# A three-layer fp32 model on one Trainium2 core: norms of the head-attention stage moved to GpSimd, and side work dealt out to other steps

## The reference

```
x = x + attn_a(layernorm(x))   # gated attention, quadratic and linear parts, width 256
x = x + ffn(layernorm(x))      # mixture of experts
x = x + attn_b(layernorm(x))   # 16 heads of 64: the "head attention"
x = x + ffn(layernorm(x))      # the same mixture of experts, same weights

layernorm: (x - mean) / sqrt(var + 1e-5)

attn_b:  q, k, v = x @ w + b (per head); attn = softmax(q k^T / 8, axis=2)
         out = concat(attn @ v) @ l_w.T + l_b

ffn:     probs = softmax(x @ Wr); the two best of 8 experts for each token
         each expert takes the first 160 tokens of a batch row that chose it
         h = relu(slots @ W1 + b1); y = h @ W2 + b2
         out = sum over the two of prob * kept * y[slot of the token]
```

## Time and profile before

| what | value |
|---|---|
| median of 3 runs | 1502.43 us (1499.57 to 1503.81) |
| span of the profiled execution | 1499.3 us |
| mean granted clock of TensorE | 0.993 of full speed |
| PE busy | 1445.1 us, 96% |
| DVE busy | 1063.7 us, 71% |
| ACT busy | 919.5 us, 61% |
| POOL busy | 280.3 us, 19% |

### The profile page before, as it was taken

How to read it: one execution, slowest core, us unless ns; L and a number is a source line. 1 busy time by engine, 2 the same in 40 slices (tenths; PEclk the granted TensorE clock), 3 DMA queues, 4 the chain that set the end, 5 groups by cost and what they waited for, 6 DMA issues and landing times.

```text
span 1499.3 us, 43267 instructions
## 1 busy us (share of the span) xinstructions
PE 1445.1 (96%) x18426; PEld 1004.5 (67%) x18426; DVE 1063.7 (71%) x2172; ACT 919.5 (61%) x1727; POOL 280.3 (19%) x325
## 2 busy tenths in 40 slices
PE   7999789999999999999999999999999999999996
PEld 6988774565677675656777756557777565467486
DVE  6884037887666679877666788776667887777754
ACT  5765566656666666566666666666666665666553
POOL 4165613013210012130000120400000213000055
PEclk9999999999999999999999999999999999999999
DMA  8501221001110011010000110110001101100002
GB/s 223 192 19 57 67 61 38 22 23 46 28 30 16 16 42 33 23 48 16 16 16 16 40 32 22 34 47 16 16 16 39 32 23 34 47 16 16 1 19 57
DMA packets 44461, 58.27 MB, mean 39 GB/s; under 512 B 8231, under 2 KB 32656, under 8 KB 44144
## 3 DMA queue, kind: packets, MB, share of 16 engines
q1 hardware_dynamic: 35120, 38.27, 9.4%
q0 software_dynamic: 9152, 17.26, 4.1%
HBM read 22.14 MB, written 19.32 MB: 28 GB/s over the span
## 4 chain that ended last, share of the span: by engine, by line
PE 86%; DVE 7%; ACT 3%; issue 2%; another core or an unknown queue 2%; DMA 0%; DVEq 0%; ACTq 0%
PE bank L1134 29%; PE bank L1147 26%; PE bank L1057 6%; PE bank L1062 4%; PE bank L1071 3%; PE bank L434 3%; PE bank L406 3%; DVE nmx L1169 3%; PE bank L1289 2%; PE bank L1285 2%; ACT prob L1178 2%; PE bank L1246 1%; ACT hT L528 1%; DVE stats L1330 1%
## 5 line engine op out<-in xcount | busy, mean ns | idle before, releaser
L1178 ACT ACTIVATE prob<-bank,nmx 128x1024 f32<-128x1024 f32 x512 | 570.3, 1114 | 427.3 <-DVE nmx L1169 426.4
L1169 DVE TENSOR_REDUCE nmx<-bank 128x1 f32<-128x1024 f32 x512 | 625.8, 1222 | 210.2 <-PE bank L1134 193.7
L1147 PE MATMUL bank<-prob,vsc 64*64 64x512 f32 x4096 | 644.9, 590 | 4.6 <-DVE ctxT L1196 2.7
L1134 PE MATMUL bank<-q,k 64*64 64x512 f32 x2048 | 530.4, 592 | 6.6 <-ACT prob L1178 5.5
L1134 PE MATMUL bank<-q,ks 64*64 64x512 f32 x2048 | 527.4, 591 | 0.0
L1147 PEld LDWEIGHTS bank<-prob,vsc 64*64 64x64 f32 x4096 | 232.3, 133 | 130.6 <-issue 64.3
L1057 PE MATMUL bank<-xT,wqkv_sb 64*64 64x256 f32 (+1 forms) x1560 | 210.3, 435 | 0.0
L1134 PEld LDWEIGHTS bank<-q,ks 64*64 64x64 f32 x2048 | 137.0, 133 | 81.0 <-issue 26.8
L1741 POOL DMA_INDIRECT yg<-yslots,row_ring x64 | 64.5, 1008 | 609.3 <-PE bank L1134 581.5
L1134 PEld LDWEIGHTS bank<-q,k 64*64 64x64 f32 x2048 | 133.9, 133 | 46.8 <-ACT prob L1178 16.6
L1057 PEld LDWEIGHTS bank<-xT,wqkv_sb 64*64 64x64 f32 x1560 | 90.3, 133 | 89.3 <-issue 39.7
(11 more groups left out here) (270 smaller groups left out, 1619.7 us busy)
## 6 DMA issues: line engine op xcount, KB each, us to landing
ks<-k SPq DMA_DIRECT2D x62, 256.0 KB
yslots<-slots_sb SPq DMA_DIRECT2D x7, 640.0 KB, 3.6
slots_sb<-xslots SPq DMA_DIRECT2D x5, 640.0 KB, 4.8
xslots<-xhat_r POOLq DMA_DIRECT2D x5, 512.0 KB, 7.3
yslots<-xhat_r POOLq DMA_DIRECT2D x5, 512.0 KB, 12.4
w_sb<-in_w SPq DMA_DIRECT2D x1, 2048.0 KB, 9.0
wqkv_sb<-in_wqkv SPq DMA_DIRECT2D x1, 2048.0 KB, 19.1
xslots<-xhat_r,row_s POOLq DMA_INDIRECT x112
```

Of the source, the lines that this page charges most:

```text
L1134: ins = nc.tensor.matmul(bank[rows(c), SC[h][n], :], kk[r, cols(2 * j + c, HD)], qst[pi % 2][r, cols(n, HALF)], start=True, stop=True)
L1147: ins = nc.tensor.matmul(bank[rows(h), CX[n], :], vsc[s][rows(r), rows(h)], prob[g % 3][h][rows(r), cols(n, HALF)], start=(j == 0 and firs ...
L1169: nc.vector.tensor_reduce(nmx[:, 2 * s + h:2 * s + h + 1], bank[:, SC[h][0]:SC[h][0] + 2, :], mybir.AxisListType.XY, ALU.max, negate=True) ...
L1178: nc.scalar.activation(prob[g % 3][h][:].rearrange("p (n c) -> p n c", c=HALF), bank[:, SC[h][0]:SC[h][0] + 2, :], ACT.Exp, bias=nmx[:, 2 ...
```

## The change

- The Newton steps and the normed rows of both norms (except the c norm of row 0) run on GpSimd, in `norm_gpsimd`: four operations a round on 128 x 8, three rounds, eight TENSOR_SCALAR of 128 x 128, and for a c norm the bias addition of 128 x 1024. VectorE keeps statistics, aggregation and the first guess, in four steps of three, three, two and no tiles.
- The c norm of row 1 has its statistics at steps 24 to 27 of block 0, those of rows 2 and 3 at steps 0 to 3 of blocks 1 and 2. The f norms begin at step 0 of block 0 and step 8 of the others.
- Chunks: in blocks 1 to 3 `xr`, `lg`, `pos` are one step later; `ln` is at steps 36 and 37 of block 0 and 9 and 10 of blocks 1 and 2; the experts begin at step 38 of block 0 and 37 of the others, and the last `answers` of block 0 is at step 0 of block 1. `slots` moves one step later in blocks 1 and 2.
- Combines: one tile a step at steps 38 to 53 (two a step in block 0).
- GpSimd's indirect DMAs: scatters and the first gathers are each held by the scores of one head, so that two in one step are half a step apart; the later gathers are at the steps in `GATHER_AT`, and the norms stand between them in GpSimd's program.

```diff
+        ROUTE_AT = [13, 14, 14, 14]
+        LN_AT = [36, 9, 9]
+        SLOTS_AT = [33, 34, 34]
+        EXPERTS_AT = [38, 37, 37]
+
         def chunks_of(b):
-            out = {13: ("xr", 0), 14: ("xr", 1), 15: ("lg", 0), 19: ("pos", 0)}
-            if b < B - 1:
-                out.update({28: ("ln", 0), 29: ("ln", 1)})
+            r = ROUTE_AT[b]
+            out = {r: ("xr", 0), r + 1: ("xr", 1), r + 2: ("lg", 0), r + 6: ("pos", 0)}
             if b == B - 1:
                 return out
+            for i in range(2):
+                out[LN_AT[b] + i] = ("ln", i)
             for i in range(3):
-                out[33 + i] = ("slots", i)
-                out[60 + i] = ("answers", i)
+                out[SLOTS_AT[b] + i] = ("slots", i)
+                out[EXPERTS_AT[b] + 3 * E + i] = ("answers", i)
             for e in range(E):
-                out[36 + 3 * e], out[37 + 3 * e], out[38 + 3 * e] = ("up", 2 * e), ("up", 2 * e + 1), ("down", e)
+                at = EXPERTS_AT[b] + 3 * e
+                out[at], out[at + 1], out[at + 2] = ("up", 2 * e), ("up", 2 * e + 1), ("down", e)
...
+                if pi % PAIRS == 0 and pi > 0:
+                    v.wait_ge(n_bias, b)
...
+        def c_bias_vector(v, step):
+            xb = xres[:, 0:T, :]
+            v.wait_ge(m_xhat, 2)
+            step.done(nc.vector.tensor_tensor(xb, xb, bl_sb[:].unsqueeze(1).to_broadcast([P, T, P]), ALU.add))
+
+        def first_norm_vector(v, step, piece):
+
+            if piece == 0:
+                aggr_vector(v, step, T)
+                newton_vector(v, step, T, NEWTON, True)
             else:
+                xhat_vector(v, T, 0, xhat, piece - 1, m_xhat)
+
+        NORM_ORDER = [("f", 0), ("c", 1), ("c", 2), ("f", 1), ("c", 3), ("f", 2), ("f", 3)]
+
+        def norm_vector(v, step, kind, b, piece):
+
+            c0, row = (T, b) if kind == "c" else (0, (b - 1) % B)
+            if piece == 0 and kind == "f" and b > 0:
+                v.wait_ge(c_res, 2 * PAIRS * b)
+            if piece < 3:
+                stats_vector(v, step, c0, row, ((0, 1, 2), (3, 4, 5), (6, 7))[piece])
+            if piece == 2:
+                aggr_tiles(v, step, c0, range(4))
+            if piece == 3:
+                aggr_tiles(v, step, c0, range(4, T))
+                guess_vector(v, step, c0)
+
+        def aggr_tiles(v, step, c0, tiles):
+            step.wait()
+            for t in tiles:
+                ins = nc.vector.bn_aggr(meanvar[:, c0 + t, :], stats[:, c0 + t, :])
+            step.done(ins)
+
+        def guess_vector(v, step, c0):
+            c = slice(c0, c0 + T)
+            step.wait()
+            step.then(nc.vector.tensor_scalar(varp[:, c], meanvar[:, c, 1], EPS, None, ALU.add))
+            step.done(nc.vector.tensor_scalar(half_var[:, c], varp[:, c], -0.5, None, ALU.mult))
+            step.then(nc.vector.tensor_scalar(newton[:, c].bitcast(I32), varp[:, c].bitcast(I32), 1, None, ALU.arith_shift_right))
+            nc.vector.tensor_tensor(rstd[:, c].bitcast(I32), magic[:, c], newton[:, c].bitcast(I32), ALU.subtract).then_inc(n_guess, 1)
...
+        def norm_gpsimd(p, step, kind, b):
+
+            c0, row, xh, done = (T, b, xhat, m_xhat) if kind == "c" else (0, (b - 1) % B, xhat_r, g_xhat)
+            c = slice(c0, c0 + T)
+            y, z = rstd[:, c], newton[:, c]
+            hold(p, n_guess, NORM_ORDER.index((kind, b)) + 1)
+            for _ in range(NEWTON):
+                step.then(nc.gpsimd.tensor_tensor(z, y, y, ALU.mult))
+                step.then(nc.gpsimd.tensor_tensor(z, z, half_var[:, c], ALU.mult))
+                step.then(nc.gpsimd.tensor_scalar(z, z, 1.5, None, ALU.add))
+                step.then(nc.gpsimd.tensor_tensor(y, z, y, ALU.mult))
+            if kind == "f" and b > 0:
+                p.wait_ge(g_sc, 256 * b)
+            elif kind == "f":
+                p.wait_ge(f_sc, 256 * (B - 1))
+            elif b == 1:
+                p.wait_ge(m_xT, 2)
+            else:
+                p.wait_ge(g_free, ln_turned(b - 2))
+            for t in range(T):
+                ins = nc.gpsimd.tensor_scalar(xh[:, t, :], row_of(row, t), meanvar[:, c0 + t, 0:1], rstd[:, c0 + t:c0 + t + 1],
+                                              ALU.subtract, ALU.mult)
+                if t % 4 == 3:
...
+                    ins.then_inc(done, 1)
+            if kind == "c":
...
+                p.wait_ge(m_xhat, 2 * (b + 1))
+                nc.gpsimd.tensor_tensor(xb, xb, bl_sb[:].unsqueeze(1).to_broadcast([P, T, P]), ALU.add).then_inc(n_bias, 1)
...
-        COMBINE = {14: (0, 0, 4), 15: (0, 4, 8), 31: (1, 0, 4), 32: (1, 4, 8)}
-        COMBINE_0 = {5: (1, 0, 0, 4), 6: (1, 0, 4, 8), 14: (1, 1, 0, 4), 15: (1, 1, 4, 8),
-                     43: (2, 0, 0, 4), 46: (2, 0, 4, 8), 52: (2, 1, 0, 4), 55: (2, 1, 4, 8)}
+        FIRST_COMBINE = {}
+        for n, at in enumerate((6, 8, 9, 10, 11, 12, 13, 14)):
+            FIRST_COMBINE[at] = (1, n // 4, 2 * (n % 4))
+        for n, at in enumerate((42, 43, 44, 45, 50, 51, 52, 53)):
+            FIRST_COMBINE[at] = (2, n // 4, 2 * (n % 4))
+        COMBINE_AT = 38
+        NORM_AT = {}
+        for kind, b, at in (("f", 0, 0), ("c", 1, 24), ("c", 2, 64), ("f", 1, 72), ("c", 3, 128), ("f", 2, 136), ("f", 3, 200)):
+            for piece in range(4):
+                NORM_AT[at + piece] = (kind, b, piece)
...
+            if b == 0 and s in FIRST_COMBINE:
+                fb, k, t = FIRST_COMBINE[s]
+                first_combine_vector(v, step, fb, k, (t, t + 1))
+            if b > 0 and COMBINE_AT <= s < COMBINE_AT + 2 * T:
+                k, t = divmod(s - COMBINE_AT, T)
+                f_combine_vector(v, step, b, k, (t,))
+            if g in NORM_AT:
+                norm_vector(v, step, *NORM_AT[g])
+            r = s - ROUTE_AT[b]
+            if 3 <= r < 6:
+                f_route_vector(v, step, b, r - 3)
+            if 7 <= r < 9:
+                f_route_vector(v, step, b, r - 4)
...
-                if s == 31:
+                if s == SLOTS_AT[min(b, B - 2)] - 2:
...
-                if s == 63 and b < B - 1:
-                    hold(sp, g_free, chunk_at(b, 62) + 1)
-                    sp.dma_start(yslots[slots, :].rearrange("(i p) c -> p i c", p=P), slots_sb[:]).then_inc(g_st, 16)
-                if s == 35 and b >= 2:
+                if g - 1 in CHUNK and CHUNK[g - 1][1:3] == ("answers", 2):
+                    n, fb = CHUNK[g - 1][0], (CHUNK[g - 1][3] - 1) % B
+                    hold(sp, g_free, n + 1)
+                    sp.dma_start(yslots[fb * SLOTS:(fb + 1) * SLOTS, :].rearrange("(i p) c -> p i c", p=P), slots_sb[:]).then_inc(g_st, 16)
+                if s == COMBINE_AT + 2 * T + 1 and b >= 2:
...
-        def paced(p, g):
-
-            hold(p, c_qk, 2 * min(g + 3, LAST + 1))
+        def paced(p, g, h=1):
+
+            hold(p, c_qk, 2 * min(g + 3, LAST + 1) - 1 + h)
+
+        GATHER_AT = [3, 4, 6, 7, 8, 9, 10, 11, 14, 15, 16, 17, 18, 19, 20, 21]
...
-                        paced(p, 31 + c)
-                    elif t % 2 == 0:
-                        paced(p, 1 + c // 2)
+                        paced(p, 33 + c)
+                    else:
+                        paced(p, 1 + c // 2, c % 2)
...
-                    elif b < B:
-                        paced(p, g0 + k * T + t)
                     c = k * T + t
+                    if b < B:
+                        if c == 2 and b < B - 1:
+                            norm_gpsimd(p, step, "c", b + 1)
+                        if c == T:
+                            norm_gpsimd(p, step, "f", b)
+                        paced(p, b * STEPS + GATHER_AT[c])
...
-                    if t % 2 == 0:
-                        paced(p, b * STEPS + 22 + (k * T + t) // 2)
+                    c = k * T + t
+                    paced(p, b * STEPS + ROUTE_AT[b] + 9 + c // 2, c % 2)
...
+        def c_gpsimd(p, step):
             first_gather(p, 1)
+            norm_gpsimd(p, step, "f", 0)
             for b in range(B - 1):
                 c_scatter(p, b)
                 if b == 0:
+                    norm_gpsimd(p, step, "c", 1)
                     first_gather(p, 2)
-                c_gather(p, b + 1, range(2))
+                c_gather(p, step, b + 1, range(2))
             c_scatter(p, B - 1)
```

More of the change, by code:

```diff
@@ L1228, in chunk_wait @@
         def chunk_wait(pe, g):
-            b = g // STEPS
-            n, kind, i = CHUNK[g]
+            n, kind, i, b = CHUNK[g]
             if kind == "xr":
@@ L1621, in c_vector @@
             nc.vector.tensor_scalar(bq, bq, HD ** -0.5, None, ALU.mult).then_inc(c_bias, 1)
-            c_norm_vector(v, step, 0, 7)
+            c_bias_vector(v, step)
             for h in range(2):
@@ L1723, in beside_last, with c_gather @@
                 hold(p, f_ytr, 3 * m + i - 4)
-        def c_gather(p, b, ks):
+        def c_gather(p, step, b, ks):
             fb = (b - 2) % B
@@ L1732, in c_gather @@
                 hold(p, f_st, 16 * (B + 1))
```

(10 more changed lines are left out.)

74 lines of the change are left out of this document (10 added, 64 removed).

## The result

The changed kernel takes 1,486.96 us (median of 4 runs, 1,483.37 to 1,490.19), the kernel before on the same chip 1,501.0 (4 runs, 1,499.25 to 1,503.81): ratio 0.9903, 95% interval 0.988 to 0.9926, so 14 us faster. The forecast was 1,491.8, its own range 1,489 to 1,494.5, the wide range 1,483.5 to 1,499.5.

A forecast was written before the change was run, and what follows sets the result against it. TensorE was taken to bound the head-attention stage, leaving only small holes to win; 7.5 + 1.2 + 4.2 - 2.3 = 10.6 us gained gave a median of 1,491.8, own range 1,489 to 1,494.5, 8-in-10 range 1,483.5 to 1,499.5.

The forecast's parts named there:

- So of the 4.2, scatters explain 1.7 and the c norm 2.5: Steps 22 to 30, blocks 0 to 2: hole of 4.2 us; moving norm work off VectorE gains 7.5 in all.
- Indirect DMAs one by one, half of 8.4: Scatters and first gathers: paired DMAs cost 8.4 us at present; spacing them gains half, +4.2.
- rival 1: Spaced indirect DMAs cost what paired ones do; 6.4 us gained, so 1,496.0; chance 0.20.
- Combines and `xr` a step later, 0.3 a block: Steps 14 and 15 lose four combine operations each on VectorE; 0.3 us a block, 1.2 gained.
- the routing pieces cost what they cost: Routing pieces move one step with the `xr` chunk in blocks 1 to 3, at no added cost.
- The bias addition, three hits of half of 1.4, -2.3: GpSimd's three long bias additions may hold back VectorE's `vsc`; about half of 1.4 us each, -2.3.
- GpSimd's rows at 0.29: Each 128x128 norm row on GpSimd takes 0.29 us, interpolated between 0.19 and 0.61.
- Rival 5: Norm rows come late for the transposes; at three times the path's time, 4 us late in three blocks, 1,504; chance 0.02.
- Steps 22 to 30 near 40: Sign: this stretch of blocks 0 to 2 falls to near 40 us from 44.
- Rival 3: The c norm's 2.5 is TensorE's lost pairing from any disturbance, not VectorE's load; 3.1 us gained, 1,499.3; chance 0.10.
- Rival 4: GpSimd keeps the ports through a burst, so `vsc` waits out rows and bias; slower, 1,510; chance 0.08.
- Rival 2: Everything goes: bias additions miss `vsc`, spaced DMAs are free; 17.1 us gained, 1,485.3; chance 0.15.

The follow-up runs named there:

- the split: Changed kernel with GpSimd's 128x1024 bias addition cut into eight of 128x128, without waits between; 1,456.03 us, ratio 0.9975 to the kernel before.

## Why the prediction was right, point by point

The direction and the wide range held, but two errors of opposite sign met in the sum; that it came out this near is luck. In the stage, 13.2 us were gained where 10.6 were forecast. By the two kinds of chip this divides into 10.8 from spacing (forecast +4.2) and 2.4 from all the rest (7.5 + 1.2 - 2.3 = 6.4), if the rest is worth as much on the one chip as on the other.

- *"So of the 4.2, scatters explain 1.7 and the c norm 2.5"*: this is the step that failed. It took the scatters' cost from block 3 and called the remainder the c norm's. The same program without late maxima has 40.53 for 43.96 in block 1 and 38.80 for 40.65 in block 3: bursts cost 3.4 in the one and 1.85 in the other. That a late maximum meets less room with the c norm beside it is my reading of the difference, not shown. The c norm, dense on VectorE but without its `ln` chunks in the stretch, costs 1.05 in three blocks, not 7.5. With them it costs more: on the chip without late maxima block 1's stretch is 1.73 longer than block 3's (40.53 and 38.80). The two `ln` chunks take 0.93 of that, by steps 9 and 10 of the changed kernel there (4.77 and 4.76 in block 1 with them, 4.30 each in block 3 without); 0.8 a block is left, 2.4 in three. Pairs have no part in it: with single DMAs the stretch is 40.53 too.
- *Indirect DMAs one by one, half of 8.4*: the present cost was mis-sized (the stage of the same program is 14.6 shorter where nothing is late; I had 8.4), and so was the part of it that goes: 10.8, not half. In the changed kernel single DMAs leave no maximum over 0.13 late in two traces of such chips. So rival 1, which had single ones as late as paired ones, is refuted, and my bound of 24 us lost was far off. I had looked at maxima only: what single DMAs do cost here, at most the 3.8, shows on TensorE in the step traced above.
- *Combines and `xr` a step later, 0.3 a block*: steps 13 to 15 did get 0.96 to 1.1 a block shorter, but not by the combines: with routing back at 13 and the combines still gone they take 15.22. They got shorter because the `lg` chunk left them for step 16, which I had not followed: steps 16 to 21 grew by 1.8, and steps 13 to 21 of the four blocks are 2.45 longer. The term was nothing, and "the routing pieces cost what they cost" was wrong. That the position of the routing does it, the run with routing at 13 shows. 0.5 a block of it is TensorE's late start beside the gather of step 16; the rest I did not trace.
- *The bias addition, three hits of half of 1.4, -2.3*: two hits, 1.75 by the split. Right. (Three times half of 1.4 is 2.1, not 2.3.)
- *GpSimd's rows at 0.29*: 0.80. The interpolation between 0.19 and 0.61 failed; GpSimd needs 2.2 times VectorE's 0.359. The Trainium skill, "GPSIMD Engine Reference", section 4.1, calls one-input operations roughly line-rate and only two-input ones twice as slow; here the one-input row is even more so than the two-input bias (2.37 to 1.22, 1.9 times). It cost nothing: the first four rows, which TensorE asks for first, end 2.0 later than I had them, and of the 5.4 to spare 3.4 were left in block 1. Rival 5 had no part.
- *Steps 22 to 30 near 40*: they came to 38.9. My floor of 39.8 held two ln chunks, and the change sends these to steps 36 and 9; that is 0.8 of the fall, and it is given back there (steps 0 to 12 of block 1 +1.2, 36 to 63 of block 0 +0.9).
- *Rival 3* (TensorE's lost pairing, set off by any disturbance) was nearer the truth on the norm than my forecast, as to the price: with VectorE as busy as before, the stretch is short once the bursts and the `ln` chunks are gone. Its mechanism was not tested. *Rival 4*: the rows hold `vsc` by 0.2 at most (0.47 for 0.29, once).
- *Rival 2* fits the time best, by compensation: bias additions did not miss `vsc`, but sending the DMAs singly was worth more than it assumed.

What stays open: why one chip starts its engines late behind indirect DMAs and another doesn't. The instructions, the DMAs' durations and the granted clock in the stage (1.00) are the same. The experiments saw two chips of the one kind and one of the other, each once, so that it is the chip, and not something else about that set of runs, is not shown. Nor was spacing alone run in the kernel before, or pairs in the changed one, on a chip where it matters; the 10.8 is a difference of differences.

## What to carry to other kernels

When a stretch is long beside two suspects, price each by a kernel that has only that one; the remainder after subtracting the first is not the second's price when both use the same room. Send indirect DMAs of GpSimd one by one between the steps of other engines: a single one cost about 0.5 us in a few steps where the result was measured, while bursts of two cost some 0.7% (10.8 us by the estimate above) there and nothing on two other chips, and fours cost 1.9% more than twos on the one where they ran. Break a long two-input GpSimd operation that may meet a two-input VectorE one, and when a hand-written order is shifted, follow every piece that shifts along.
